# Turning two of four tiles with VectorE and 16 small transfers in place of TensorE

## What is computed

```python
x = _layernorm(x + attn(x))            # x: 8192 tokens of 512 numbers
x = _layernorm(x + ffn(x))
# attn: feats = AB * exp(x @ (ab*proj).T - 0.5*|x|^2*ab^2) / sqrt(512);  feats @ weights.T
# ffn:  real = x @ cos(theta + theta_noise);  imag = x @ sin(phi + phi_noise)
#       sqrt(real*real + imag*imag)
```

## Time and profile before

| | |
|---|---|
| time, median of 3 runs | 727.88 us (727.87 to 728.87) |
| profiled execution: time | 727.47 us |
| profiled execution: first to last instruction (span) | 725.7 us |
| TensorE busy | 708.1 us, 98% of the span |
| VectorE busy | 564.7 us, 78% |
| ScalarE busy | 489.5 us, 67% |
| GpSimd busy | 276.4 us, 38% |
| DMA queue q1 (all of SP's transfers) | 24.5% of 16 engines' span |

### The profile page before, as it was taken

How to read it: one execution, slowest core, us unless ns; L and a number is a source line. 1 busy time by engine, 2 the same in 40 slices (tenths; PEclk the granted TensorE clock), 3 DMA queues, 4 the chain that set the end, 5 groups by cost and what they waited for, 6 DMA issues and landing times.

```text
span 725.7 us, 10939 instructions
## 1 busy us (share of the span) xinstructions
PE 708.1 (98%) x3228; PEld 584.4 (81%) x3228; DVE 564.7 (78%) x964; ACT 489.5 (67%) x758; POOL 276.4 (38%) x464
## 2 busy tenths in 40 slices
PE   8989999999999999999999999999999999999993
PEld 7867888888888888888888888888888888888873
DVE  5889789797777868778786877869687777877686
ACT  6836757593957769395775939677594866757463
POOL 5764026606144250614416052341605235160525
PEclk9999999999999999999999999999999999999997
DMA  9752031320503232050322305032130503200011
GB/s 311 213 130 72 1 112 71 120 62 21 168 15 116 72 103 70 15 173 15 116 72 74 99 15 173 15 116 72 58 115 15 164 24 116 69 32 29 1 58 58
DMA packets 32753, 60.80 MB, mean 84 GB/s; under 512 B 3168, under 2 KB 3168, under 8 KB 32736
## 3 DMA queue, kind: packets, MB, share of 16 engines
q1 hardware_dynamic: 31584, 58.50, 24.5%
q0 software_dynamic: 1152, 2.10, 1.7%
HBM read 43.78 MB, written 16.81 MB: 83 GB/s over the span
## 4 chain that ended last, share of the span: by engine, by line
PE 89%; DVE 6%; ACT 2%; DMA 1%; issue 1%; POOL 0%; SPq 0%; POOLq 0%; DVEq 0%; ACTq 0%
PE token_ps L898 9%; PE token_ps L900 9%; PE token_ps L899 9%; PE project_ps L751 7%; PE project_ps L749 7%; PE project_ps L750 7%; PE token_ps L802 7%; PE token_ps L801 7%; PE token_ps L803 7%; PE project_ps L899 3%; PE project_ps L900 3%; PE project_ps L898 3%; PE turn_ps L812 3%; PE token_ps L830 1%; PE token_ps L829 1%; PE token_ps L831 1%
## 5 line engine op out<-in xcount | busy, mean ns | idle before, releaser
L399 POOL TENSOR_TENSOR late<-late 128x1024 f32<-128x1024 f32 x29 | 71.5, 2467 | 307.6 <-ACT late L667 307.6
L749 PE MATMUL project_ps<-xT_hi,gs_hi 128*128 128x512 f32 x248 | 100.1, 404 | 0.6 <-DVE expo L1008 0.6
L801 PE MATMUL token_ps<-W_hi,F_hi 128*128 128x512 f32 x256 | 99.7, 389 | 0.0
L803 PE MATMUL token_ps<-W_hi,F_lo 128*128 128x512 f32 x256 | 99.6, 389 | 0.0
L802 PE MATMUL token_ps<-W_lo,F_hi 128*128 128x512 f32 x256 | 99.6, 389 | 0.0
L751 PE MATMUL project_ps<-xT_hi,gs_lo 128*128 128x512 f32 x248 | 97.2, 392 | 0.0
L750 PE MATMUL project_ps<-xT_lo,gs_hi 128*128 128x512 f32 x248 | 96.7, 390 | 0.0
L667 ACT ACTIVATE late<-late 128x1024 f32<-128x1024 f32 x56 | 59.3, 1059 | 36.7 <-DVE late L1388 32.0
L582 ACT ACTIVATE late<-late 128x1024 f32<-128x1024 f32 x29 | 30.8, 1062 | 76.4 <-POOL late L399 76.4
L642 ACT ACTIVATE z<-z,shift,rstd 128x512 f32<-128x512 f32 x56 | 45.2, 807 | 40.5 <-POOL shift L394 40.5
L1126 DVE TENSOR_TENSOR z<-token_ps,x_tok 128x512 f32<-128x512 f32 x64 | 44.2, 690 | 31.3 <-PE token_ps L803 28.0
(11 more groups left out here) (212 smaller groups left out, 1799.5 us busy)
## 6 DMA issues: line engine op xcount, KB each, us to landing
x_tok<-in_x SPq DMA_DIRECT2D x16, 1024.0 KB, 5.5
out_tokens<-o_tile SPq DMA_DIRECT2D x62, 256.0 KB, 2.2
plain_xT_lo<-in_xT SPq DMA_DIRECT2D x14, 1024.0 KB, 5.3
norm_bc<-token_norms SPq DMA_DIRECT2D x15, 256.0 KB, 3.1
plain_T_hi<-in_gsT SPq DMA_DIRECT2D x4, 256.0 KB, 4.0
z<-in_wT SPq DMA_DIRECT2D x4, 256.0 KB, 4.3
plain_T_lo<-in_xT SPq DMA_DIRECT2D x1, 1024.0 KB, 7.7
plain_T_hi<-in_theta SPq DMA_DIRECT2D x4, 256.0 KB, 6.6
```

The source lines that it names most:

```text
L399: pool.tensor_tensor(parts[:, p, :, 0, :], parts[:, p, :, 0, :], parts[:, p, :, 1, :], ALU.add).then_inc(sum_made, 2)
L749: nc.tensor.matmul(o, gs_hi[:, c, cols], rhs_hi[:, c, :], start=(c == 0), stop=False)
L801: nc.tensor.matmul(o, F_hi[:, c, cols], W_hi[:, c, :], start=(c == 0), stop=False)
L803: return nc.tensor.matmul(o, F_lo[:, c, cols], W_hi[:, c, :], start=False, stop=(c == C - 1))
```

## The change

In blocks 2 to 14 the tiles 2 and 3 are no longer turned by TensorE. VectorE transposes both, in place of the 128x128 turn, in squares of 32x32 (one instruction of 128x1024, `turn_squares`), which turns each square but leaves it in its own 32 partitions. SP then moves the squares to the right partitions: for each of 4 source and 4 target groups of 32 partitions one transfer of 32x8x32 numbers, into `zT_raw[:, 1]` (`move_squares`). The halves of pair 1 thus lie in SBUF and not in `turn_ps`. `norm1(3)` on ScalarE is moved ahead of the first features.

```diff
@@ SP
+            def move_squares(b):
+                sp.wait_ge(squares_turned, b - PLAIN + 1)
+                for i in range(P // 32):
+                    for k in range(P // 32):
+                        src = turned_squares[32 * i:32 * i + 32].rearrange("r t (c k s) -> r (t c) k s", c=C, s=32)
+                        dst = zT_raw[32 * k:32 * k + 32, 1, 0:4 * Q].rearrange("r (c i s) -> r c i s", c=2 * C, s=32)
+                        sp.dma_start(dst[:, :, i, :], src[:, :, k, :]).then_inc(halves_moved, 16)
                     store_out(b - 1, 2)
                     store_out(b - 1, 3)
+                if moved:
+                    move_squares(b)
                 if ahead:
                     sp.wait_ge(project_done, C * (b + 3))
                     sp.dma_start(xT_raw[:, :, :], xT_blocks[b + 2]).then_inc(xT_loaded, 16)
@@ ScalarE
+                def round_moved_first():
+                    act.wait_ge(halves_moved, MOVE_CREDIT * (s + 1))
+                    nc.scalar.activation(zT_hi[:, 1, 0:2 * Q], zT_raw[:, 1, 0:2 * Q], ACT.Copy).then_inc(halves_hi_made, 1)
+                def round_moved_sums():
+                    act.wait_ge(half_sums_made, 8 * s + 8)
+                    nc.scalar.activation(zT_hi[:, 1, 2 * Q:7 * Q], zT_raw[:, 1, 2 * Q:7 * Q],
+                                         ACT.Copy).then_inc(half_sums_hi_made, 1)
                     round_first(0)
+                    norm1(3)
                     features(C * (b + 2), 0, 0)
                     round_second(0)
-                    norm1(3)
                     features(C * (b + 2) + 1, 1, 1)
                     round_half_sums(0)
                     features(C * (b + 2) + 2, 2, 0)
-                    round_first(1)
-                    round_second(1)
                     features(C * (b + 2) + 3, 3, 1)
                     copy_first(0)
-                    round_half_sums(1)
                     load_table(ACT.Sqrt)
+                    round_moved_first()
                     if ahead:
...
+                        sum_square(b + 3, 0, slot, 1 - slot)
+                        sum_square(b + 3, 1, slot, 1 - slot)
+                    round_moved_sums()
@@ TensorE
-                    turn(b, 2)
-                    turn(b, 3)
@@ VectorE
+                def turn_squares():
+                    dve.wait_ge(out_made, C * (b - 1) + 3)
+                    dve.wait_ge(z_made, C * b + 4)
+                    nc.vector.transpose(turned_squares, z[:, 2:4, :]).then_inc(squares_turned, 1)
+                def moved_half_sums():
+                    dve.wait_ge(halves_moved, MOVE_CREDIT * (s + 1))
...
                     split_first(0)
                     next_exponent(b, slot, 1)
+                    turn_squares()
                     split_second(0)
                     half_sums(0)
                     next_exponent(b, slot, 2)
                     split_half_sums(0)
                     split_feature_pair(C * (b + 2) + 1, 0)
                     next_exponent(b, slot, 3)
-                    split_first(1)
-                    split_second(1)
-                    half_sums(1)
                     join_u(0)
                     join_v(0)
                     join_c22(0)
                     join_w(0)
-                    split_half_sums(1)
+                    moved_half_sums()
+                    split_moved_first()
                     join_c11(0)
+                    split_moved_sums()
                     split_feature_pair(C * (b + 2) + 3, 1)
```

More of the change, by code:

```diff
@@ L95, in build @@
         parts = late.rearrange("p (q i t) d -> p q i t d", q=2, i=2)
+        turned_squares = late[:, 4:6, :]
         o_tile = sb("o_tile", [P, 2, D])
@@ L221, in build @@
         JOIN_CREDIT = 3
-        HALF_SUMS = ["S1", "S2", "S3", "S4"]
+        HALVES = ["A11", "A12", "A22", "S1", "S2", "S3", "S4"]
+        MOVED_HALVES = ["A11", "A12", "S4", "A22", "S1", "S2", "S3"]
+        MOVE_CREDIT = 16 * (P // 32) ** 2
         QUARTER_SUMS = ["T1", "T4", "T3", "T2"]
@@ L284, in _, with step @@
             fetch_norms(2, 0)
-            def step(b, slot, ahead, first=False):
+            def step(b, slot, ahead, first=False, moved=False):
                 if not first:
@@ L313, in _ @@
                 for slot in range(2):
-                    step(pair * 2 + slot, slot, True)
+                    step(pair * 2 + slot, slot, True, moved=True)
             for slot in range(2):
-                step(NB - 2 + slot, slot, False)
+                step(NB - 2 + slot, slot, False, moved=(slot == 0))
             store_out(NB - 1, 0)
@@ L886, in second_step, with half @@
                     last.then_inc(phase_done, 1)
-            def half(p, k):
+            def half(p, name, moved):
+                k = (MOVED_HALVES if moved else HALVES).index(name)
                 cols = [slice(k * Q + i * P, k * Q + (i + 1) * P) for i in range(H)]
@@ L911, in pair_products @@
                 join_order = JOIN_ORDER if more else JOIN_ORDER_LAST
+                moved = more and p == 1
                 for name in QUARTER_ORDER if more else QUARTER_ORDER_LAST:
                     if name == "M1":
-                        pe.wait_ge(halves_lo_made, 4 * s + 2 * p + 1)
+                        pe.wait_ge(halves_lo_made, 3 * s + 2 * p + 1)
                         if p == 0:
@@ L918, in pair_products @@
                             pe.wait_ge(joined, joins_done(b, 0, join_order, "C11"))
-                        quarter_product(token_ps[0][:, :], half(p, 0), quarter(cos_hi, cos_lo, 0))
+                        quarter_product(token_ps[0][:, :], half(p, "A11", moved), quarter(cos_hi, cos_lo, 0))
                     if name == "M6":
@@ L925, in pair_products @@
                             pe.wait_ge(joined, joins_done(b, 0, join_order, "U"))
-                        quarter_product(token_ps[1][:, :], half_sum(p, "S2"), quarter_sum("T2"))
+                        quarter_product(token_ps[1][:, :], half(p, "S2", moved), quarter_sum("T2"))
                     if name == "M7":
@@ L931, in pair_products @@
                             pe.wait_ge(joined, joins_done(b, 0, join_order, "V"))
-                        quarter_product(token_ps[2][:, :], half_sum(p, "S3"), quarter_sum("T3"))
+                        quarter_product(token_ps[2][:, :], half(p, "S3", moved), quarter_sum("T3"))
                     if name == "M5":
@@ L945, in pair_products @@
                     if name == "M4":
-                        pe.wait_ge(halves_lo_made, 4 * s + 2 * p + 2)
+                        if not moved:
+                            pe.wait_ge(halves_lo_made, 3 * s + 2 * p + 2)
                         if p == 1:
@@ L950, in pair_products @@
                             pe.wait_ge(expo_made, C * (b + 2) + 3)
-                        quarter_product(project_ps[0][:, :], half(p, 2), quarter_sum("T4"))
+                        quarter_product(project_ps[0][:, :], half(p, "A22", moved), quarter_sum("T4"))
                     if name == "M3":
@@ L956, in pair_products @@
                             pe.wait_ge(expo_made, C * (b + 2) + 4)
-                        quarter_product(project_ps[1][:, :], half_sum(p, "S4"), quarter(low_sin_hi, low_sin_lo, 0))
+                        quarter_product(project_ps[1][:, :], half(p, "S4", moved), quarter(low_sin_hi, low_sin_lo, 0))
             def step(b, more, behind_plain=False):
@@ L1347, in half_sums @@
                     tt(S4, A12, S2, ALU.subtract).then_inc(half_sums_made, 1)
+                def half_sums(p):
+                    sum_halves(p, turn_ps[0][:, 0:Q], turn_ps[0][:, Q:2 * Q], zT_raw[:, p, 6 * Q:7 * Q], turn_ps[1][:, Q:2 * Q],
+                               *[zT_raw[:, p, (3 + k) * Q:(4 + k) * Q] for k in range(4)])
                 def split_half_sums(p):
```

34 lines of the change are left out of this document (20 added, 14 removed).

## The result

The changed kernel takes 749.08 us (median of 4 runs, 748.06 to 752.19) where the kernel before takes 728.27 (4 runs, 727.87 to 728.87): 1.0294 times as long, with a 95% interval of 1.0276 to 1.0312. It is slower by 21 us; the forecast was 3.4 us faster. The profiled execution took 752.19 us, 3.1 above the median, and showed a mean clock of 0.986.

The account below looks back on a forecast made before the run. TensorE's own work was taken to bound the 13 changed blocks: 0.89 us saved minus a 0.63 stall leaves 0.26 a block, 3.4 us in all, giving a median of 724.5 us; range 716 to 749.

Parts of the forecast that it names:

- The pace of its issues ... 0.33 each; larger ones 0.47 apart. I take 410.3: SP's sixteen transfers: issued 0.33 to 0.47 us apart from 401.7, squares landed between 407.9 and 410.9, taken as 410.3.
- The cover behind them: Squares landed 1.8 us before VectorE, free of join_w at 412.08, would need them, so the transfers were hidden.
- The packets must not be slower than the issues: DMA engines, 128-byte runs: 27 ns a packet, 0.44 us a transfer, just under the 0.47 between issues.
- The first rival: Squares land late and VectorE waits at the first moved sum; 740 as its middle, chance 0.30.
- From there each us costs 13 us in all: Each us that the squares land after 412.34 adds 13 us to the kernel, over 13 blocks.
- The saving, 0.89 a block: TensorE without the eight transposes of turns 2 and 3 saves 0.89 us a block, 11.6 us over 13 blocks.
- The transpose, 1.2: VectorE's 128x1024 transpose takes 1.2 us, leaving 0.65 us of cover before M6(0) would wait.
- The chain behind `join_w`, 0.63: VectorE's and ScalarE's sums, splits, rounding and join_c11 delay M1(1) and M6(1), stalling TensorE 0.63 us a block.
- The third rival, the full gain: Chain of sums, split and join 0.6 us shorter, so no stall is left: 716.3 us, chance 0.12.
- The load of `xT_raw`: Behind the 16 issues on SP's queue, issued about 409.2, landing 414.5; ScalarE needs it at 414.67, nothing waits longer.
- the 412.34 from which the first rival decides: Landing instant of the squares, 412.08 + 0.26, from which their lateness sets the outcome.
- the 33 that the prediction had weighed and set aside: Estimate of 33 us for 16 transfers one after the other, at a fixed 2.0 us each, losing 20 us a block.

Follow-up runs that it names:

- e8: Changed kernel with four 32x1024 SBUF-to-SBUF transfers, plus twelve of 32x256 to an unread HBM buffer, in place of the sixteen; single run, 725.49 us.
- e2: Changed kernel with its sixteen transfers each as 32 runs of 1 KB in place of 256 of 128 bytes, columns misordered; 741.43 us.
- e1: Changed kernel with four transfers of 32x1024, each within its own 32 partitions, in place of sixteen, so numbers are misplaced; 726.23 us.
- e10: e7 with copy_first(0) on ScalarE moved ahead of features(3); 720.05 us, 0.989 of the kernel before.
- e3: Changed kernel with eight of the sixteen transfers sent from GpSimd's queue; 729.18 us, 1.0017 of the kernel before.
- e7: e3 with pair 1's sums ahead of join_c22 and join_w on VectorE, and ScalarE rounding them after one square sum, not two; 724.59 us.
- e4: Changed kernel with norm1(3) ahead of round_first(0) on ScalarE and turn_squares ahead of split_first(0) on VectorE; 735.45 us.
- e5: Changed kernel with join_c11(0) on VectorE ahead of the moved sums; 747.45 us.
- e11: The order of e7 with all sixteen transfers on SP's queue; 755.54 us, 1.0376 of the kernel before.

## Why the prediction was wrong

- **"The pace of its issues ... 0.33 each; larger ones 0.47 apart. I take 410.3": this step failed.** The issues were 0.65 apart, so the squares landed 11.75 us after the first issue and not 8.6. The cover behind them was 1.8 us, and 3.15 - 1.8 = 1.35 is the wait that the profile shows (1.28 in the mean). I took the price of one kind of transfer from rows of two others, of four partitions and of loads from HBM, and called their span the range; e8 and e2 show that the kind that was to be priced lies outside it. The dearest issue in the trace of before was passed over too (end of this section).
- **"The packets must not be slower than the issues": right in its outcome.** The first rival was put on this term, 45 ns a packet; the rival held, by another mechanism. The packets were not the limit (28.6% busy, and e2).
- **"From there each us costs 13 us in all": mis-sized.** A mean wait of 1.28 would have given 13 x (1.28 - 0.26) = 13 us by it, and 741. An ordinary block lost 1.52 against e1 (44.10 - 42.58). It is made up so: ahead of M1(1) TensorE stands idle 1.41 and 1.61 in turn where it does 0.25 and 0.35 in e1, 1.21 more, and M6(1) starts 1.88 after M1(1) in place of the 1.58 of e1, 0.30 more. The 0.30 is in the rows above: ScalarE, late too, had two square sums ahead of the sums' rounding, which could have begun at 383.87 and began at 384.22. Three blocks lost 1.84 more than an ordinary one: their stall is 0.74 longer in the mean, and the other 1.1 goes with half the clock (below). In the first two of them SP's sixteen issues took 10.95 and 11.44 in place of 10.44, why is open.
- **The saving, 0.89 a block: right** (0.90 in e10). The transpose, 1.2: right (1.24), and M6(0) does not wait, so its cover held.
- **The chain behind `join_w`, 0.63: nearly right.** With transfers in time (e1) a block is 42.58, so the chain costs 42.58 - 41.76 = 0.82, and 0.08 was left of the gain, not 0.26. From the first moved sum to M1(1) I had 2.92 us; e1 shows 2.93 (its first sum starts at 370.76, M1(1) at 373.69). What I had too small is spread: M1(1) starts 0.41 later than the matmuls ahead of it would let it (373.28) where I had 0.34, in every second block 0.10 later still, and M6(1) 1.58 after it where I had 1.54.
- **The third rival, the full gain, was out of reach in this order**, but not in another: e10 has it but for one pause.
- The load of `xT_raw`, behind the 16 issues on SP's queue, went out at 381.28 and nothing waited for it, as forecast.

The issue that was passed over, a load of 1 MB, 3.3 us behind the two of the earlier trace rows from which I took 0.47:

```profile
5.11 0.62 SPq L274 DMA_DIRECT2D plain_T_lo<-in_xT  x1
```

The next issue follows it 0.66 later (at 5.77). By this pace the last of sixteen would start at 401.7 + 9.9 = 411.6 and land between 412.8 and 413.8, beyond the 412.34 from which the first rival decides. It is another kind as well, but it would have moved the range over the line. That the landings lie beside the next issues was right: each took 1.9 us, and sixteen took 11.75 from the first issue to the last landing, far from the 33 that the prediction had weighed and set aside. The fixed 2.0 us of a transfer that it took there from the Trainium skill, DMA: Bandwidth & Descriptors, Anatomy of one DMA, is given by the page for transfers issued from GpSimd; the 1.9 us measured here on SP's queue is near it.

What stays of the three parts for an ordinary block: -0.90 for the turns, +0.82 for the chain, +1.52 for the lateness, together 1.44. The lateness is shown by e1 and, with all squares in their right places, by e3; that the chain's order is what costs the 0.82 is shown by e7 and e10, which both changed it.

## What to carry to other kernels

Count the transfers of one queue and price each by its issue, by a row of the same kind (same ends, same number of partitions); if the trace has none, look for its dearest issue too (0.62 here), and let the range go beyond the nearest rows on the side where the answer turns. Against transfers that land late the second queue did most: e3 returned 20 of 21 us, the earlier start of e4 14, and the other order of those who wait (e5) only moved the wait. And once a wait is gone, look for the next at the end of the block and follow it back over the engine without idle time to the wait that began it; in e7 it lay 15 us ahead on another engine, and one moved instruction (e10) was worth 4.5 us.

## What the hardware showed that I had not expected

The price of an issue on SP's queue, each as total over number:

| transfer | issue, us | from |
|---|---|---|
| SBUF to SBUF, 32 partitions, 128-byte runs | 0.65 | changed kernel |
| the same, 1 KB runs | 0.63 | e2 |
| the same, 4 KB runs | 0.62 | e1 |
| SBUF to HBM, 32 partitions, 1 KB runs | 0.47 | e8 |
| SBUF to HBM, 4 partitions, small | 0.33 | |
| HBM to SBUF, 128 partitions, 1 MB, one issue | 0.62 | before, L274 |
| SBUF to SBUF by GpSimd, 128-byte runs | 0.58 | e3 |

TensorE's clock fell around the three longest stalls of the changed kernel. Windows of the changed kernel around the M1(1) of an early block: TensorE busy, clock, DMA share, GB/s.

```profile
206.00:208.00 2.00, 0.00 (x0) 0.89 0.92 313
208.00:209.00 1.00, 0.98 (x2) 0.50 0.77 297
209.00:210.00 1.00, 1.00 (x4) 0.50 0.00 0
210.00:211.00 1.00, 1.00 (x4) 0.51 0.00 0
211.00:212.00 1.00, 1.00 (x5) 1.00 0.00 0
```

```profile
208.01 0.80 PE L928 MATMUL token_ps<-cos_hi,zT_hi 128*128 128x512 f32 x1 [2.41 <-DVE late L1427]
208.61 0.63 PE L929 MATMUL token_ps<-cos_lo,zT_hi 128*128 128x512 f32 x1
...
210.74 0.50 PE L928 MATMUL token_ps<-T_hi,zT_hi 128*128 128x512 f32 x1
```

After 2.41 us without work the granted clock is 0.50, the 1.2 GHz level, for some 3 us: six matmuls take 2.73 us from first to next where they take 1.88 with M6(1)'s own wait in the block above. It was so in the three blocks with idle stretches of 2.2 to 2.4 us, and in none of the ten with 1.4 to 1.6; in the other two of the three the clock fell only 1.7 and 1.0 us after TensorE had started again. The length of the stall does not decide alone: in e11 the clock fell 1.0 us after a stall of 2.23 us (M1(1) at 161.19), and stayed at 1.00 around a longer one of 2.68 (M1(1) at 207.52). The three blocks of the changed kernel make up 5.5 us of its profiled execution (3 x (3.28 - 1.44)), the longer stall and the clock together, and a different number of them in different executions may be why its time lies 3.1 above the median; that was not tested.
